# The masked attention layer: the second bank of a score step is computed from a copy of keys and queries whose row halves are exchanged

## The reference

```
Q, K, V = split(q @ Wq.T), split(k @ Wk.T), split(v @ Wv.T)
scores = einsum('bhqd,bhkd->bhqk', Q, K) * scale
scores = where(mask, -inf, scores)
out = einsum('bhqk,bhkd->bhqd', softmax(scores), V)
```

## Time and profile before

| | before |
|---|---|
| median of three runs | 1785.07 us |
| profiled execution, its time | 1786.3 us |
| its span in the profile | 1783.6 us |
| TensorE busy | 1568.4 us (88%) |
| VectorE busy | 1344.5 us (75%) |
| ScalarE busy | 1174.2 us (66%) |
| granted TensorE clock, mean | 0.936 of 2.4 GHz |
| masked layer, first piece to last product | 1329.7 to 1697 us |

### The profile page before, as it was taken

The page is one execution under the profiler, slowest core; times in us unless marked ns, Lnnn a source line. Parts: engine busy times, 40 slices in busy tenths (PEclk is TensorE's granted clock), DMA queues, the critical chain, the costliest instruction groups (busy, mean ns, idle before and its releaser), DMA issues.

```text
span 1783.6 us, 45505 instructions
## 1 busy us (share of the span) xinstructions
PE 1568.4 (88%) x15403; PEld 652.6 (37%) x15403; DVE 1344.5 (75%) x2285; ACT 1174.2 (66%) x2201; POOL 142.1 (8%) x231
## 2 busy tenths in 40 slices
PE   5789999978778999996997799999778999999867
PEld 3422222246232222224675122222453333333345
DVE  4689999745769999974784899999347777777358
ACT  3368888842545888883894488888443666666636
POOL 4000000012000000002121000000100000000012
PEclk9889999989897999997899699999887999999979
DMA  8922222205542222220115322222172211111001
GB/s 275 292 77 76 91 76 75 83 1 150 182 134 61 91 76 75 90 60 12 48 61 154 118 76 76 91 75 62 38 230 62 62 60 60 60 61 60 29 13 36
DMA packets 91729, 156.46 MB, mean 88 GB/s; under 512 B 15623, under 2 KB 41758, under 8 KB 91646
## 3 DMA queue, kind: packets, MB, share of 16 engines
q1 hardware_dynamic: 86846, 145.54, 26.4%
q0 software_dynamic: 1792, 4.66, 0.8%
q10 hardware_dynamic: 3008, 5.13, 0.8%
HBM read 119.13 MB, written 35.14 MB: 86 GB/s over the span
## 4 chain that ended last, share of the span: by engine, by line
PE 55%; DVE 18%; issue 11%; DMA 6%; SPq 5%; ACT 2%; POOL 1%; DVEq 0%; ACTq 0%; POOLq 0%
PE pv_bank L1512 17%; DVE mx L1063 12%; PE exp_ring L1478 10%; PE score_ring L1464 9%; DMA qp<-ms 4%; PE exp_ring L1493 4%; PE score_ring L1664 3%; PE exp_ring L1675 3%; PE exp_ring L1496 2%; DMA k_d<-k2c 2%; SPq L529 2%; PE score_ring L1403 1%; PE score_ring L1577 1%; PE exp_ring L1410 1%; ACT early L835 1%
## 5 line engine op out<-in xcount | busy, mean ns | idle before, releaser
L835 ACT ACTIVATE early<-exp_ring 128x512 f32<-128x512 f32 (+1 forms) x1728 | 930.6, 597 | 328.4 <-PE exp_ring L1478 172.7
L1063 DVE TENSOR_REDUCE mx<-score_ring 128x2 f32<-128x802 f32 (+2 forms) x832 | 764.5, 966 | 71.2 <-PE score_ring L1464 56.3
L1464 PE MATMUL score_ring<-kp,qp 64*128 64x401 f16 (+4 forms) x2688 | 503.1, 350 | 71.8 <-DVE mx L1063 47.6
L1512 PE MATMUL pv_bank<-early,vg 128*32 128x256 f32 (+1 forms) x6912 | 557.6, 393 | 2.9 <-issue 2.0
L1478 PE MATMUL exp_ring<-qp,kp 64*128 64x512 f16 (+2 forms) x1312 | 366.2, 390 | 17.9 <-DMA qp<-ms 16.2
L1464 PEld LDWEIGHTS score_ring<-kp,qp 64*128 64x128 f16 (+2 forms) x2688 | 155.8, 100 | 270.3 <-DVE mx L1063 160.0
L1512 PEld LDWEIGHTS pv_bank<-early,vg 128*32 128x32 f32 (+1 forms) x6912 | 140.5, 108 | 209.9 <-issue 122.4
L1478 PEld LDWEIGHTS exp_ring<-qp,kp 64*128 64x128 f16 (+2 forms) x1312 | 92.0, 95 | 308.0 <-ACT early L835 241.9
L661 POOL COPY vg<-v_all 128x416 f32 (+1 forms) x48 | 25.4, 533 | 884.4 <-PE pv_bank L1512 833.4
L1493 PE MATMUL exp_ring<-qp,kp 64*64 64x512 f16 x832 | 86.4, 403 | 6.9 <-issue 3.7
L1056 DVE CUSTOM_DVE_ANT_0 wfcT<-score_ring,mask_add 128x802 f16<-128x802 f32 x64 | 63.6, 994 | 32.2 <-PE score_ring L1464 25.6
(11 more groups left out here) (241 smaller groups left out, 1243.9 us busy)
## 6 DMA issues: line engine op xcount, KB each, us to landing
kp<-k_d SPq DMA_DIRECT2D x128, 400.2 KB, 3.2
qp<-q_d SPq DMA_DIRECT2D x160, 256.0 KB, 3.3
k_d<-k1c SPq DMA_DIRECT2D x32, 400.2 KB, 8.2
ctxT<-ctxT_d SPq DMA_DIRECT2D x12, 800.5 KB, 6.0
k_d<-k2c SPq DMA_DIRECT2D x16, 400.2 KB, 9.2
q_d<-qp ACTq DMA_DIRECT2D x1, 4096.0 KB, 23.0
ctxT_d<-ctxT SPq DMA_DIRECT2D x4, 800.5 KB, 9.3
o_all<-in_ctx SPq DMA_DIRECT2D x4, 768.0 KB
```

The source lines that it names most:

```text
L835: act.activation(pt[g][0:rows_, 2 * h:2 * h + 2, :], bank[0:rows_, :].rearrange("p (i q) -> p i q", q=S), ACT.Exp).then_inc(exped, 1)
L1063: dve.tensor_reduce(dst, src, AX.X, ALU.max).then_inc(score_free, 1)
L1464: ins = pe.matmul(pa[slot][q, z, 0:w], qp1[par][rows_, i, qt * P + q.start:qt * P + q.stop], kp1[par][rows_, at:at + w], start=True, stop= ...
L1512: ins = pe.matmul(po[R * j:R * j + R, 0:S], vg[par][0:rows_, s, j, :], pt[g][0:rows_, j, :], start=(s == 0), stop=(s == r.kt - 1))
```

## The change

In the masked layer `pass1` now also loads a second copy of the unit's keys and queries, with the two halves of the partitions exchanged: what lies in partitions 0 to 63 is loaded to 64 to 127, and the other way round. These are four more DMAs a unit, of 64 partitions each, on SP's queue behind the two of `pass1`; they go to memory that the masked layer doesn't otherwise use (`kpx` in `v_loc` and `on_loc`, `qpx` in `w_up`). In `piece` the bank `z` = 1 reads this copy: the same head's numbers from the other half of the partitions. The four matmuls of a piece then lie in the array's four different quarters. TensorE waits for the additional loads (`in1x`) ahead of a unit's first piece, and adds to `passed_pe` once a piece where it did so once a bank.

```diff
@@ -298,6 +298,9 @@
+        kpx = [m.bitcast(F16)[:, 0:S2] for m in (v_loc[:, :, :, :].rearrange("p b k d -> p (b k d)"),
+                                                 on_loc[:, :, :].rearrange("p t d -> p (t d)"))]
+        qpx = [m[:, :].bitcast(F16).rearrange("p (i q) -> p i q", q=S) for m in w_up]
@@ -503,6 +506,10 @@
             def pass1(r, n, par):
                 sp.dma_start(kp1[par][:, 0:r.nk], k_d[r.index][n]).then_inc(in1[par], 16)
                 sp.dma_start(qp1[par][:, :, :], q_units[n]).then_inc(in1[par], 16)
+                if r.mask:
+                    for h in range(PAIRS):
+                        sp.dma_start(kpx[par][r.rows(1 - h), :], k_d[r.index][n, r.rows(h), :]).then_inc(in1x[par], 16)
+                        sp.dma_start(qpx[par][r.rows(1 - h), :, :], q_units[n, r.rows(h)]).then_inc(in1x[par], 16)
@@ -1452,18 +1459,23 @@
                     if j == 0:
                         pe.wait_ge(in1[par], IN_DMAS * (r.u0 + n - par + 2))
+                        if r.mask:
+                            pe.wait_ge(in1x[par], 2 * IN_DMAS * (n - par + 2))
                     qt, banks = r.step(j)
                     w = r.chunks[banks[0][1]][1]
+                    if r.mask:
+                        pe.sem_inc(passed_pe, 1)
                     for z in (half, 1 - half):
                         i, c = banks[z]
                         at, rows_ = r.chunks[c][0], r.rows(i // 2)
-                        if r.mask:
-                            pe.sem_inc(passed_pe, 1)
+                        q_now, k_now = qp1[par], kp1[par]
+                        if r.mask and z:
+                            rows_, q_now, k_now = r.rows(1 - i // 2), qpx[par], kpx[par]
                         for t in range(2 if r.mask else 1):
                             q = slice(2 * R * t, 2 * R * t + 2 * R) if r.mask else slice(0, P)
                             ins = pe.matmul(pa[slot][q, z, 0:w],
-                                            qp1[par][rows_, i, qt * P + q.start:qt * P + q.stop],
-                                            kp1[par][rows_, at:at + w], start=True, stop=True)
+                                            q_now[rows_, i, qt * P + q.start:qt * P + q.stop],
+                                            k_now[rows_, at:at + w], start=True, stop=True)
                     ins.then_inc(score, 1)
```

More of the change, by code:

```diff
@@ L346, in flamingo @@
         prep_w, prep_p0, f_ve, f_rs, r_acc = [sem(n) for n in ("prep_w", "prep_p0", "f_ve", "f_rs", "r_acc")]
-        ctx_in, ctx_out, c_ld, k_out, in1, in2, m_in, e_w = [
-            [sem(f"{n}_{i}") for i in range(2)] for n in ("ctx_in", "ctx_out", "c_ld", "k_out", "in1", "in2", "m_in", "e_w")]
+        ctx_in, ctx_out, c_ld, k_out, in1, in1x, in2, m_in, e_w = [
+            [sem(f"{n}_{i}") for i in range(2)] for n in ("ctx_in", "ctx_out", "c_ld", "k_out", "in1", "in1x", "in2", "m_in", "e_w")]
         ln_st, ln_mv, ln_ve, ln_rs, ln_xn, ln_t, ln_xt = [
```

## The result

The changed kernel takes 1775.56 us (median of 9 runs, 1772.12 to 1782.3); the kernel before, in runs beside it, 1784.7 us (9 runs). The ratio is 0.9948, with a 95% interval of 0.9937 to 0.9958: 9.1 us faster. The forecast was 1768, its range 1761 to 1781.

A forecast was written before the change was run, and what follows sets the result against it. TensorE was taken as the bound, with VectorE at 76%. 14.0 + 0.8 + 3.1 + 0.5 - 1.3 = 17.1 us off the profiled 1786.3 gives 1769.2, a median of 1768 us; range 1761 to 1781.

The forecast's parts named there:

- first rival: In the masked layer's units, VectorE and the stagger eat more of the gain: 0.5 us a unit, 1777 us, chance 0.20.
- third rival: On SP's queue, half-rate added loads delay the `ms` rows about 2.5 us a unit: 1810 us; milder 1789; chance 0.07 together.
- What a piece gains: In a piece's score matmuls, the second pair starts beside the first: TensorE's share falls from 0.44 to 0.27 us.
- single steps: Steps of a unit with one piece: ScalarE's loop holds them at 1.40 us, gaining 0.07 each, 0.42 for six.
- double steps: Steps 2, 4 and 6 of a unit, two pieces each: 1.60, 1.84 and 1.60 us, gaining 0.29, 0.05 and 0.29.
- The choice between the two staggers: How closely a piece's four matmuls start: 1.22 us a unit by the skill, 0.92 with 0.06 us stagger; 1.0 taken.
- the row after a wait: Profile row where four score matmuls take 0.53 us after a wait, otherwise 0.50; read as 0.06 us or more of stagger.
- the low clock: In the first unit's first steps, about four pieces gain 0.33 instead of 0.17 us: 0.5 us.
- The 23 pieces: At the layer's start, pieces without a second pass beside them gain 0.27 us in each of 11.5 cycles: 3.1 us.
- The start of the added loads: The added loads delay TensorE's first piece from 1329.68 to 1331 us: 1.3 us lost, between 0 and 3.1.
- The added loads in the loop: Loads ahead of the `ms` rows on SP's queue just fit: no cost, with a bound of 0.5 us a unit, 7 us.
- step 12: Last step of a unit; in steps 10 to 12 `ms` rows end the wait, only VectorE's earlier start counts: gain 0.17 us.

The follow-up runs named there:

- e1: The changed kernel without the four additional loads, bank 1 reading another head's rows of the original tables (output not the reference's): 1763.21 us, ratio 0.9888.
- e2: The changed kernel with the additional loads and their wait kept, but both banks reading the original tables: 1791.05 us, ratio 1.0035.
- e3: The changed kernel with the four additional loads of a unit issued behind the `ms` rows and `pass2` instead of ahead: 1767.36 us, ratio 0.9906.
- e5: e3 with unit 0's first four pieces on the original tables, the wait ahead of the fifth, unit 1's loads behind unit 0's `pass2`: 1763.88 us, ratio 0.9888.
- e7: The changed kernel with the two additional loads of keys ahead of the `ms` rows and the two of queries behind: 1765.9 us, ratio 0.9901.

## Why the prediction came out as it did

The direction was right and the time inside the range, but 8 us above the forecast. It fell on the time of the first rival, and for another reason: that rival had VectorE and the stagger eat the gain; in fact the added loads did, which is the third rival's mechanism, in a milder form than the one priced there. (Its 1777 us are 9.5 us off the profiled execution; off the median, as the forecast is, they are 1775.6.) So it is partly luck that the time lies in the range: the upper end was drawn for a rival that didn't come true, and an error of some 11 us in the loads was made smaller by one of 3 us the other way in the matmuls.

1. **What a piece gains: right.** Four matmuls beside each other (0.04 us apart), single steps 1.40 us by ScalarE's loop, double steps 1.63, 1.83 and 1.64 us against 1.60, 1.84 and 1.60. The steps worked out and the rows of the trace agree to 0.04 us.
2. **The choice between the two staggers: mis-sized.** The forecast took 1.0 us a unit, near the 0.92 of the row after a wait. With no loads in the way (e1) a unit gains 21.22 - 19.97 = 1.25 us. The 0.06 us of stagger was set against the double steps, and there it isn't: a second piece's four matmuls start within 0.01 us, after a wait too (1490.24). In the single steps the last starts 0.04 us behind the first, which costs nothing under ScalarE's 1.40. The Trainium skill ("TensorE: Matmul & The Clock Gate", the mechanism of row and column tiling) has them about 4 ns apart, from which the prediction's estimate was 1.22; the traces agree, with 0.01 us for all four and 1.25 us a unit in e1. Over units 0 to 12 e1 gains 16.1 us, where the forecast had 13.0 and 0.5 for the low clock. Units 13 to 15 bring 2.4 us (63.8 to 61.5 from the first fills of unit 13 to the last product), where it had 1.0 and 0.8.
3. **The 23 pieces: right.** Forecast 3.1 us, measured 25.24 - 22.25 = 3.0 in e1. In the changed kernel only 1.2 is left, since this stretch ends with the wait of 1.81 us for unit 0's `ms` rows.
4. **The start of the added loads: too low.** Forecast 1.3 us lost, between 0 and 3.1. The changed kernel starts 2.9 us later than before, e2 3.0: at the upper bound. The step took it that a load with half the bytes ends earlier. The last one landed 11.18 us after its issue, where the full-size load that was the sixth on the queue before took 10.9.
5. **The added loads in the loop: failed.** "That just fits: nothing" rested on three numbers. The loads were taken at the rate of those of 128 partitions; the rate row shows 180 to 300 GB/s for them instead of 330 to 400. The `ms` rows were set at 5.1 us after SP issues the first load, a time that the faster pieces shorten to 4.7. And their packets were read as moving from 1504.1 to 1504.8 us, where the earlier trace rows has them at 1504.4 and 1505.0. The third rival's condition, loads that end 1.4 us or more after the `ms` issue, was met in most units (1.35 to 1.74 us), but where it cost anything the fills then came 0.2 to 0.8 us late and not 1.5. The bound of 0.5 us a unit held in units 2 to 12, 20.36 - 19.97 = 0.39. It didn't hold in units 0 and 1: they lost 2.1 and 1.3 us, of which 1.7 are unit 0's step 12 with the stop of 1.92 us, and 1.3 the clock's drop in the first two steps of unit 1. The pieces ahead of unit 0 lost another 1.8 us, where SP itself was still issuing loads. The sum had none of these.

Together: without the loads 21 us, with them 9. Between the traces of the changed kernel and e1 the loads cost 13.1 us (478.6 - 465.5; 12.4 by the medians): 3.7 are the first piece (2.9 against the kernel before), 1.8 the first pieces, 2.1 unit 0, 1.3 unit 1, and 11 x 0.39 = 4.3 the units 2 to 12. e3 takes back 8 of the 12 by order alone. A further gain of e5 is not shown beyond the noise.

What stays open: first, whether the `ms` rows wait behind the loads' packets in one queue or share the DMA engines with them. e3 and e7 move the loads in time and in the queue at once; issuing the rows from another engine's queue, which would tell the two apart, wasn't tried. Second, why a load of half the partitions moves at some 60% of the rate isn't shown by any run. Third, that the loads cause the stop in unit 0 is argued from where it occurs, not shown.

## What to carry to other kernels

When matmuls have few rows, give neighbours different quarters of the array even if it takes a second copy of the operands; here this brought 21 of 1785 us. Then look at what the copy's loads stand in front of: a small transfer at the end of a chain goes first, and bulk that is due a unit later goes behind it. And price added loads against the time scale after the change, since a slack that is read from the old trace shrinks with the very gain that one is after. Last, once another engine's loop sets the step, spread the work evenly over the steps: here a step with no piece and one with a single piece both took 1.40 us.

## What the runs showed of the hardware that was not expected

- DMAs of 64 partitions move more slowly than those of 128: in the rate row 180 to 300 GB/s against 330 to 400. The packets are of the same sizes, but each takes longer. One of 3202 bytes takes 127 ns (median) from 1497.6 to 1499.1 us, among loads of 128 partitions, and 215 from 1500.0 to 1502.4, among those of 64; one of 2048 bytes takes 84 and 160 ns. The Trainium skill ("DMA: Bandwidth & Descriptors", the table of recommendations) says that both halves spread over all 16 engines, which the prediction took for the full rate; the same row says that two such transfers serialize, and to use one of 128 partitions. The trace agrees with the advice: the two halves together take longer than the whole.
- At the backlog of the layer's start, a load of 128 KB took 11.18 us from issue to landing in the changed kernel, and one of 256 KB in the same place of the queue 10.9 us before.
- TensorE's granted clock stayed at 1.00 from 1385 to 1650 us when its busy share was 93% instead of 98%, and was at 1.2 GHz from 1381.1 to 1384.5, after 1.92 us without a matmul.
